# Attention over edges: the product of keys and queries stays in PSUM, and the values' product stands between the two score products

## The chip, the cores and the metric

The kernel runs on one core of one Trainium2 chip (trn2). The metric is the device time of one execution in microseconds, as the median of several runs. Engines are named as in the profile: PE is TensorE, DVE is VectorE, ACT is ScalarE, POOL is GpSimd, SP is SyncE; "q" behind a name means its sequencer, which issues DMAs.

## The reference

A network of four graph blocks over 6,250 nodes and 106,250 edges, 128 features wide, each block followed by a residual and a layer norm. The change is in the last one, attention over edges with 8 heads of 16:

```python
Q = (x @ WQ).reshape(N, H, dh)
K = (x @ WK).reshape(N, H, dh)
V = (x @ WV).reshape(N, H, dh)
Eh = (edge_attr @ WE).reshape(-1, H, dh)
score = K[src] * Q[dst] / jnp.sqrt(jnp.float32(dh)) * Eh
score = jnp.exp(jnp.clip(score.sum(-1, keepdims=True), -5.0, 5.0))
msg = V[src] * score
wV = jax.ops.segment_sum(msg, dst, num_segments=N)
Z = jax.ops.segment_sum(score, dst, num_segments=N)
h_attn = (wV / (Z + ATTN_EPS)).reshape(N, D)
```

## The kernel before

The edges are sorted by the tile (125 nodes) of their target node and laid out in 272 groups of 512 slots, four to each of 128 partitions. Groups beyond the edges that there are hold blanks. `attn` runs once, late in the program, as one loop over the groups on all engines at once: 34 trips of `Q` = 8 groups on DVE, PE and SP; on POOL it is written out. Most buffers form rings of `RING` = 4 groups.

For group g, in the order in which its data move:

- POOL (L748) issues four indirect DMAs; each gathers 128 rows of keys and values (1 KB each) from `kv_table` into `kv_r`. Before a group's first gather it waits for `attn_ready` of group g - 4.
- SP (L663) loads the group's 256 KB of edge terms into `eh_r`, also once `attn_ready` tells that group g - 4 is done, and (L650) the row of target nodes of group g + 4 into `row_b`.
- DVE makes the one-hots `oht_r` of group g + 2 from `row_b` (`q_one_hots`, L1564), and counts `q_hot`.
- PE (`q_of`, L868) waits for `q_hot`, multiplies these with the tile of queries into PSUM bank 6 + g % 2, and counts `q_rows`. So a group's queries stand in PSUM two laps before they are used.
- DVE: `times_q` (L1581) waits for the four gathers (`kv_in`) and for `q_rows`, and multiplies the keys with the queries. Before the change the product goes to `gath[:, 6 + q % 2]` in SBUF. `times_eh` (L1587) multiplies it with the edge terms in place, `head_sums` (L1591) sums the 16 features of each head, `clamp` (L1597) limits the sums and counts `score_ready`.
- ACT takes the exponent (L1135, `exp_done`). Ahead of it in its queue stand the one-hots of the target nodes for group g + 2 (L1119, L1123), which wait for `attn_sums` of group g - 2.
- DVE: `times_scores` (L1602), one lap later, multiplies the values with the exponent into `vs_r` and counts `attn_ready`.
- PE (`sums`, L876) waits for `attn_ready` and the one-hots and adds up the group per node in PSUM; in PE's order `sums` of group g - 1 stands behind `q_of` of group g + 2. DVE adds the result to the node sums three laps later (`add`, L1576).

Each engine works strictly in the order in which its part is written. DVE's order within a lap is `lap` (the lines from 1609 on). Instructions of DVE that depend on one another wait through `sch` (semaphore `score_chain`).

Of the kernel before, what the change touches and what calls it, by code (L numbers as in the profile page):

```python
# [19 lines left out]
ALU, ACT = mybir.AluOpType, mybir.ActivationFunctionType  # L20
# [3 lines left out]
N, E, D = 6250, 106250, 128  # L24
# [12 lines left out]
RING = 4  # L37
# [179 lines left out]
def program(nc, A):  # L217
    ctx = ExitStack()
    with ctx:
# [55 lines left out]
        ps = ctx.enter_context(nc.psum_tensor("ps", [P, 8, 512], F32))  # L275
# [123 lines left out]
        kv_r = part_of_big([P, RING, PER, 2 * D], NA * NODES_PAD)  # L399
        eh_r = part_of_big([P, RING, PER, D])  # L400
# [883 lines left out]
        def _(dve):  # L1284
            ch, sch = Chain(dve, dve_chain), Chain(dve, score_chain)
# [272 lines left out]
            def attn(n):  # L1558
# [3 lines left out]
                def q_one_hots(i, q):  # L1562
# [3 lines left out]
                                      .rearrange("p (u j) -> p j u", j=UNIT), part[0:NT, 0:1], None,  # L1566
                                      ALU.is_equal).then_inc(q_hot, 1)

                def quads(q):
                    return gath[:, 6 + q % 2, :].rearrange("p (k f) -> p k f", f=D)  # L1570

# [6 lines left out]
                def times_q(g, trip, q):  # L1578
                    dve.wait_ge(kv_in[q], 16 * PER * trip)
                    dve.wait_ge(q_rows, g + 1)  # L1580
                    sch.mark(dve.tensor_tensor(quads(q), kv_r[:, q, :, 0:D],  # L1581
                                               ps[:, 6 + q % 2, :].rearrange("p (k f) -> p k f", f=D), ALU.mult))

                def times_eh(trip, q):
                    dve.wait_ge(eh_in[q], 16 * trip)
                    sch.wait()
                    sch.mark(dve.tensor_tensor(quads(q), quads(q), eh_r[:, q, :, :], ALU.mult))  # L1587

                def head_sums(q):
                    sch.wait()  # L1590
# [9 lines left out]
                def times_scores(g, q):  # L1600
                    dve.wait_ge(exp_done, g + 1)
                    dve.tensor_tensor(vs_r[:, q, :, 0:D].rearrange("p k (h d) -> p k h d", d=DH),  # L1602
                                      kv_r[:, q, :, D:2 * D].rearrange("p k (h d) -> p k h d", d=DH),
                                      vs_r[:, q, :, D:SUMS_W].unsqueeze(3).to_broadcast([P, PER, HEADS, DH]),
                                      ALU.mult).then_inc(attn_ready, 1)

                def lap(i, first, last):
                    ch.trip(i, Q)
                    sch.trip(i, 3 * Q)
                    if not first:  # L1610
                        ch.k -= lag
                        at_ = tiles_of(DVE_E, ATT_D, i * Q - lag, Q)
                    else:
                        at_ = (0,) * lag + tuple(tiles_of(DVE_E, ATT_D, 0, Q - lag))
                    for q in range(Q):
                        g, r, trip = i * Q + q, q % RING, i * (Q // RING) + q // RING + 1
                        times_q(g, trip, r)
                        if not (last and q >= Q - 2):
                            q_one_hots(i + (q + 2) // Q, (q + 2) % Q)
                        times_eh(trip, r)  # L1620
                        head_sums(r)
                        clamp(r)
                        if not (first and q == 0):
                            times_scores(g - 1, (q - 1) % RING)
                        if not (first and q < lag):
                            add(g - lag, (q - lag) % RING, at_[q])
                q_one_hots(0, 0)
                q_one_hots(0, 1)
                laps(dve, TRIPS, lap)
                ch.k += lag  # L1630
                ch.leave(TRIPS, Q)
# [244 lines left out]
```

## Time and profile before

| | us |
|---|---|
| median of 3 runs | 11,246.82 |
| lowest and highest | 11,230.78, 11,254.05 |
| span of the profiled execution, first to last instruction | 10,395.6 |
| the attention loop in it | 8,817 to 10,301 |

The profiled execution is told by its span alone; the difference to the median, some 851 us, lies outside the first and the last instruction. A span is read against a span, and a run's time against a run's time. The page lists the instruction groups by busy time, with the idle time of the engine before them and what ended it. The stretches of the trace give each engine's busy time from one time to another, the time line every instruction with its start and duration. Gathers by POOL are rows of L748: the row is the time in which POOL makes the transfer's descriptors, not the transfer itself.

### The profile page before, as it was taken

Reading aid. Unit: us, or ns where it says so; the run is one execution under the profiler, and the core shown is the slowest. Engines: PE = TensorE matmul, PEld = TensorE weight load, DVE = VectorE, ACT = ScalarE, POOL = GpSimd, SP = SyncE. Lnnn points to the kernel's source line nnn. Section 1 sums busy time; section 2 is a strip of 40 time slices with the busy share of each in tenths; the row PEclk is TensorE's granted clock in tenths of the full one; section 3 lists DMA queues with packets and bytes.
Section 4 is the critical chain, followed back from the end, with each engine's and each line's share of the span. In section 5 each row is a group of like instructions: output and inputs, shape, how many; then the busy total and the mean of one; then the engine's idle time right before and its main releaser. Section 6 shows DMA issues by size and latency. Waiting matters only on the chain.

```text
span 10395.6 us, 235883 instructions
## 1 busy us (share of the span) xinstructions
PE 7622.6 (73%) x62128; PEld 6495.8 (62%) x62129; DVE 7083.8 (68%) x16991; ACT 3619.7 (35%) x7576; POOL 4980.3 (48%) x4705
## 2 busy tenths in 40 slices
PE   4799990388787887884689777777877875666664
PEld 3567660277675776763578676766766765556553
DVE  5577770266766667666666579789798797666664
ACT  0122220230612604404520454644645544444443
POOL 0677776337054072270036037056074173777772
PEclk7555555699899998996899899999999998666665
DMA  8767664997584884960599489598796894666666
GB/s 338 198 211 213 214 208 33 101 280 244 197 293 130 296 258 156 329 190 21 159 326 421 188 323 364 214 337 303 263 352 248 307 364 157 165 162 164 161 162 78
DMA packets 1747195, 2371.76 MB, mean 228 GB/s; under 512 B 516388, under 2 KB 1046151, under 8 KB 1746651
## 3 DMA queue, kind: packets, MB, share of 16 engines
q1 hardware_dynamic: 1292446, 1275.33, 39.4%
q0 software_dynamic: 318912, 1049.17, 31.1%
q10 hardware_dynamic: 135677, 45.42, 1.9%
q8 instruction: 64, 1.05, 0.0%
q14 instruction: 96, 0.79, 0.0%
HBM read 1485.10 MB, written 955.49 MB: 235 GB/s over the span
## 4 chain that ended last, share of the span: by engine, by line
PE 19%; DVE 8%; POOL 7%; issue 6%; ACT 4%; DMA 4%; SPq 2%; DVEq 2%; ACTq 0%; POOLq 0%
PE ps L836 8%; POOL big L748 6%; PE ps L858 5%; PE ps L855 4%; DVE gath L1516 3%; ACT gath L1109 3%; DMA big<-kv_table,src_at 2%; SPq L622 2%; ACT gath L1088 1%; DVE gath L1587 1%; DVE heads L1591 1%; ACT big L1241 0%; DMA big<-rec 0%; DVE gath L1602 0%; DVEq L509 0%
## 5 line engine op out<-in xcount | busy, mean ns | idle before, releaser
L738 POOL DMA_INDIRECT gath<-msg_units,unit_at_d x2176 | 2341.0, 1076 | 3287.8 <-DMA msg_units<-gath 2605.4
L858 PE MATMUL ps<-onehot,gath 128*128 128x125 f32 x17408 | 2476.3, 287 | 636.9 <-ACT gath L1109 356.1
L858 PEld LDWEIGHTS ps<-onehot,gath 128*128 128x128 f32 x17408 | 2118.7, 193 | 994.4 <-issue 536.9
L836 PE MATMUL ps<-big,onehot 125*128 x29376 | 1921.2, 223 | 713.1 <-DVE onehot L1477 466.9
L836 PEld LDWEIGHTS ps<-big,onehot 125*128 125x128 bf16 x29376 | 1806.3, 97 | 830.8 <-issue 788.0
L1088 ACT ACTIVATE gath<-ps 128x512 f32<-128x512 f32 x2448 | 1425.3, 597 | 1212.3 <-PE ps L836 1013.0
L1477 DVE TENSOR_SCALAR onehot<-row_b,part 125x512 bf16<-125x512 uint8 x2448 | 1136.4, 482 | 690.7 <-PE ps L836 686.4
L1509 DVE TENSOR_TENSOR onehot<-iota,node_d 128x500 f32<-128x500 f32 x2176 | 1464.7, 674 | 173.4 <-PE ps L858 109.7
L748 POOL DMA_INDIRECT big<-kv_table,src_at x1088 | 1085.5, 998 | 537.2 <-issue 291.8
L710 POOL DMA_INDIRECT rec<-big,idx_ring x832 | 973.6, 1170 | 282.8 <-issue 239.9
L1109 ACT ACTIVATE gath<-gath 128x512 f32<-128x512 f32 x1088 | 685.6, 630 | 941.6 <-DVE gath L1516 941.6
L1528 DVE TENSOR_TENSOR big<-big,ps 128x125 f32 x2176 | 608.9, 280 | 391.9 <-PE ps L858 383.0
L868 PE MATMUL ps<-big,weights 125*128 x2176 | 467.0, 382 | 397.5 <-DVE weights L1564 397.5
L1516 DVE TENSOR_TENSOR gath<-gath,big 128x512 f32<-128x512 f32 x1088 | 742.9, 683 | 21.4 <-DMA gath<-msg_units,unit_at_d 21.1
L868 PEld LDWEIGHTS ps<-big,weights 125*128 125x128 f32 x2176 | 404.7, 278 | 460.4 <-issue 460.3
L876 PE MATMUL ps<-gath,onehot 128*125 128x136 f32 x2176 | 515.7, 409 | 121.6 <-DVE gath L1602 110.3
L1160 ACT ACTIVATE big<-ps,feats 128x250 f32 x125 | 53.9, 470 | 1502.7 <-PE ps L923 1502.4
L1119 ACT ACTIVATE onehot<-iota,weights 128x125 f32<-128x125 f32 x1088 | 344.7, 388 | 659.5 <-PE ps L876 612.3
L876 PEld LDWEIGHTS ps<-gath,onehot 128*125 128x125 f32 x2176 | 451.6, 296 | 180.8 <-issue 137.5
L1581 DVE TENSOR_TENSOR gath<-big,ps 128x512 f32<-128x512 f32 x272 | 186.8, 687 | 527.3 <-DMA big<-kv_table,src_at 518.3
L816 PE MATMUL ps<-weights,big 128*128 128x128 f32 x1664 | 419.7, 432 | 94.6 <-DMA gath<-in_attr_t 55.1
L738 POOL DMA_INDIRECT big<-rec,unit_at_s x136 | 138.8, 1021 | 713.9 <-DMA rec<-gath 636.4
(218 smaller groups left out, 9000.0 us busy)
## 6 DMA issues: line engine op xcount, KB each, us to landing
msg_units<-gath SPq DMA_DIRECT2D x2176, 256.0 KB, 2.2
big<-ea_units SPq DMA_DIRECT2D x1088, 256.0 KB
ea_units<-rec SPq DMA_DIRECT2D x16, 4352.0 KB, 54.4
rec<-gath SPq DMA_DIRECT2D x272, 256.0 KB, 6.2
big<-rec SPq DMA_DIRECT2D x272, 256.0 KB, 3.8
big<-in_attr_t SPq DMA_DIRECT2D x208, 256.0 KB
rec<-big SPq DMA_DIRECT2D x1, 43296.0 KB, 152.1
gath<-msg_units,unit_at_d POOLq DMA_INDIRECT x2176, 5.3
```

Source lines behind the costliest of these rows:

```text
L710: pool.indirect_dma_start(rec, bass.IndirectOffsetOnAxis(ap=idx_ring[:, q, k:k + 1], axis=0), rec_r[:, q, k, :], None).then_inc(rec_out[q] ...
L738: pool.indirect_dma_start(att_slot(q) if way == "attr" else gath[:, q, :], None, units, bass.IndirectOffsetOnAxis(ap=unit_at[w][:, g:g + 1 ...
L748: pool.indirect_dma_start(kv_r[:, q, k, :], None, table["kv"], bass.IndirectOffsetOnAxis(ap=src_at[:, g * PER + k:g * PER + k + 1], axis=0))\
L836: ins = pe.matmul(ps[:, r, c], hots_t[0:NT, r, c], upper[0:NT, ds(at_[q] + b, D)], start=b == NA * NODES_PAD, stop=b == LOW)
L858: ins = pe.matmul(ps[:, RING + r, 0:NT], unit_ring[:, q, j, :], hots[:, r, j, :], start=j == 0, stop=j == UNIT - 1)
L868: last = pe.matmul(ps[:, 6 + q % 2, k * P:(k + 1) * P], oht_r[0:NT, q % 2, k, :], big[0:NT, ds(at_ + RE * NODES_PAD, P)], start=True, stop ...
L876: last = pe.matmul(ps[0:NT, q, 0:SUMS_W], hots[:, q, k, :], vs_r[:, q, k, :], start=k == 0, stop=k == PER - 1)
L1088: act.activation(unit_ring[:, q, :, :], ps[:, q % RING, :].rearrange("p (k f) -> p k f", f=D), ACT.Copy).then_inc(evicted, 1)
L1109: act.activation(gath[:, q, :], gath[:, q, :], ACT.Relu).then_inc(msg_ready, 1)
L1477: dve.tensor_scalar(hots_t[0:NT, r, :].rearrange("p (j u) -> p j u", u=P), row_b[0:NT, k, q % RING * GSLOTS:(q % RING + 1) * GSLOTS] .rear ...
L1509: dve.tensor_tensor(hots[:, r, :, :], iota[:, 0:NT].unsqueeze(1).to_broadcast([P, UNIT, NT]), node[w][:, ds(g * UNIT, UNIT)].unsqueeze(2). ...
L1516: dve.tensor_tensor(gath[:, q, :], gath[:, q, :], ea_r[:, q, :], ALU.add).then_inc(msg_sum, 1)
```

## The change

Three things change, all in DVE's part of `attn`; no other engine's instructions change. `times_q` writes its product back into the PSUM bank that it read the queries from. `times_eh` reads it there and writes `gath` in SBUF, from where the head sums go on as before. And in a lap `times_scores` of the group before moves up to stand between these two products, while the one-hots of group g + 2 move down behind `times_eh`: these release PE to overwrite the same bank.

```diff
+                def q_ps(q):
+                    return ps[:, 6 + q % 2, :].rearrange("p (k f) -> p k f", f=D)
...
-                    sch.mark(dve.tensor_tensor(quads(q), kv_r[:, q, :, 0:D],
-                                               ps[:, 6 + q % 2, :].rearrange("p (k f) -> p k f", f=D), ALU.mult))
+                    sch.mark(dve.tensor_tensor(q_ps(q), kv_r[:, q, :, 0:D], q_ps(q), ALU.mult))
...
-                    sch.mark(dve.tensor_tensor(quads(q), quads(q), eh_r[:, q, :, :], ALU.mult))
+                    sch.mark(dve.tensor_tensor(quads(q), q_ps(q), eh_r[:, q, :, :], ALU.mult))
...
                         times_q(g, trip, r)
+                        if not (first and q == 0):
+                            times_scores(g - 1, (q - 1) % RING)
+                        times_eh(trip, r)
                         if not (last and q >= Q - 2):
                             q_one_hots(i + (q + 2) // Q, (q + 2) % Q)
-                        times_eh(trip, r)
                         head_sums(r)
                         clamp(r)
-                        if not (first and q == 0):
-                            times_scores(g - 1, (q - 1) % RING)
```

DVE in a lap in the middle of the loop, before. The rows are, in order, the product with the queries, the one-hots (written to a part of `weights`), the product with the edge terms, head sums, clamp, the values' product (written to a part of `gath`), and the addition to the node sums (two rows).

```order
L1581 TENSOR_TENSOR gath<-big,ps 128x512 [waits q_rows,kv_in0]
L1564 TENSOR_SCALAR weights<-row_b,part 125x512 [waits q_row_in6]
L1587 TENSOR_TENSOR gath<-gath,big 128x512 [waits score_chain,eh_in0]
L1591 TENSOR_REDUCE heads<-gath 128x32 [waits score_chain]
L1597 TENSOR_SCALAR heads<-heads 128x32 [waits score_chain]
L1602 TENSOR_TENSOR gath<-big,gath 128x4x128 [waits exp_done]
L1576 ISA [waits dve_chain,attn_sums]
L1576 TENSOR_TENSOR big<-big,ps 125x136
```

The same lap after, three lines further down in the file:

```order
L1584 TENSOR_TENSOR ps<-big,ps 128x512 [waits q_rows,kv_in0]
L1604 TENSOR_TENSOR gath<-big,gath 128x4x128 [waits exp_done]
L1589 TENSOR_TENSOR gath<-ps,big 128x512 [waits score_chain,eh_in0]
L1564 TENSOR_SCALAR weights<-row_b,part 125x512 [waits q_row_in6]
L1593 TENSOR_REDUCE heads<-gath 128x32 [waits score_chain]
L1599 TENSOR_SCALAR heads<-heads 128x32 [waits score_chain]
L1579 ISA [waits dve_chain,attn_sums]
L1579 TENSOR_TENSOR big<-big,ps 125x136
```

The values' product, with its wait for the exponent of the group before, has moved from the sixth place to the second, and the one-hots from the second to the fourth; the first product now writes `ps`, and the product with the edge terms reads it.

DVE in the last lap and behind it, where there are no one-hots left to make, before:

```order
L1581 TENSOR_TENSOR gath<-big,ps 128x512 [waits q_rows,kv_in3]
L1587 TENSOR_TENSOR gath<-gath,big 128x512 [waits score_chain,eh_in3]
L1591 TENSOR_REDUCE heads<-gath 128x32 [waits score_chain]
L1597 TENSOR_SCALAR heads<-heads 128x32 [waits score_chain]
L1602 TENSOR_TENSOR gath<-big,gath 128x4x128 [waits exp_done]
L1576 ISA [waits dve_chain,attn_sums]
L1576 TENSOR_TENSOR big<-big,ps 125x136
L1602 TENSOR_TENSOR gath<-big,gath 128x4x128 [waits exp_done]
```

And after:

```order
L1584 TENSOR_TENSOR ps<-big,ps 128x512 [waits q_rows,kv_in3]
L1604 TENSOR_TENSOR gath<-big,gath 128x4x128 [waits exp_done]
L1589 TENSOR_TENSOR gath<-ps,big 128x512 [waits score_chain,eh_in3]
L1593 TENSOR_REDUCE heads<-gath 128x32 [waits score_chain]
L1599 TENSOR_SCALAR heads<-heads 128x32 [waits score_chain]
L1579 ISA [waits dve_chain,attn_sums]
L1579 TENSOR_TENSOR big<-big,ps 125x136
L1604 TENSOR_TENSOR gath<-big,gath 128x4x128 [waits exp_done]
```

Here too the values' product of the group before moves up; that of the last group stands alone behind the loop in both.

## Rows read from the trace of the kernel before

**Rows 1.** The page: its first line, and L1581 among the costliest groups.

```profile
span 10395.6 us, 235883 instructions
...
L1581 DVE TENSOR_TENSOR gath<-big,ps 128x512 f32<-128x512 f32 x272 | 186.8, 687 | 527.3 <-DMA big<-kv_table,src_at 518.3
```

**Rows 2.** Stretches: from:to, length, busy us (count) by engine, clock, DMA, GB/s.

```profile
8830.00:10130.00 1300.00, 876.87 (x3973) 767.18 (x3973) 835.72 (x1739) 541.71 (x1494) 996.56 (x996) 0.68 0.63 163
10130.00:10300.00 170.00, 90.04 (x350) 78.35 (x350) 75.85 (x158) 44.73 (x123) 79.06 (x83) 0.57 0.94 103
```

**Rows 3.** Waits, 8830 to 10130 us: waiter <- releaser: us, times, longest.

```profile
DVE gath L1581 <- DMA big<-kv_table,src_at: 441.3, 220, 6.2
...
POOL big L748 <- issue: 269.3, 884, 0.3
...
POOL big L748 <- DVE gath L1602: 34.1, 112, 0.3
```

**Rows 4.** Groups by line, 8830 to 10130 us: busy us, mean ns | idle before.

```profile
L748 POOL DMA_INDIRECT big<-kv_table,src_at x996 | 997.0, 1001 | 303.5 <-issue 269.3 <-DVE gath L1602 34.1
...
L1581 DVE TENSOR_TENSOR gath<-big,ps 128x512 f32<-128x512 f32 x249 | 171.0, 687 | 447.0 <-DMA big<-kv_table,src_at 441.3 <-issue 5.5
L1587 DVE TENSOR_TENSOR gath<-gath,big 128x512 f32<-128x512 f32 x249 | 170.8, 686 | 0.0
L1591 DVE TENSOR_REDUCE heads<-gath 128x32 f32<-128x512 f32 x249 | 170.8, 686 | 8.6
L1602 DVE TENSOR_TENSOR gath<-big,gath 128x512 f32<-128x512 f32 x248 | 169.6, 684 | 0.0
L1564 DVE TENSOR_SCALAR weights<-row_b,part 125x512 f32<-125x512 uint8 x249 | 122.7, 493 | 0.0
...
L1597 DVE TENSOR_SCALAR heads<-heads 128x32 f32<-128x32 f32 x249 | 50.5, 203 | 8.7
```

**Rows 5.** Time line at 9083 us: start us, us, engine, line, operation.

```profile
9082.77 0.69 DVE L1581 TENSOR_TENSOR gath<-big,ps 128x512 f32<-128x512 f32 x1 [1.03 <-DMA big<-kv_table,src_at]
9083.37 0.48 DVE L1564 TENSOR_SCALAR weights<-row_b,part 125x512 f32<-125x512 uint8 x1
9083.77 0.68 DVE L1587 TENSOR_TENSOR gath<-gath,big 128x512 f32<-128x512 f32 x1
9083.90 1.37 POOL L748 DMA_INDIRECT big<-kv_table,src_at  x1 [0.30 <-issue]
...
9085.30 0.68 DVE L1602 TENSOR_TENSOR gath<-big,gath 128x512 f32<-128x512 f32 x1
9085.57 1.23 POOL L748 DMA_INDIRECT big<-kv_table,src_at  x1 [0.30 <-issue]
```

**Rows 6.** Time line at 9432 us, a lap with a quick landing.

```profile
9431.69 0.69 DVE L1591 TENSOR_REDUCE heads<-gath 128x32 f32<-128x512 f32 x1
9432.18 0.95 POOL L748 DMA_INDIRECT big<-kv_table,src_at  x1 [0.30 <-issue]
...
9433.38 0.58 SPq L663 DMA_DIRECT2D big<-rec  x1
...
9435.03 0.69 DVE L1581 TENSOR_TENSOR gath<-big,ps 128x512 f32<-128x512 f32 x1 [1.64 <-DMA big<-kv_table,src_at]
...
9435.93 1.00 POOL L748 DMA_INDIRECT big<-kv_table,src_at  x1 [0.30 <-issue]
9436.03 0.68 DVE L1587 TENSOR_TENSOR gath<-gath,big 128x512 f32<-128x512 f32 x1
```

**Rows 7.** Time line at 9086 us, an earlier load of edge terms.

```profile
9086.14 0.58 SPq L663 DMA_DIRECT2D big<-rec  x1
...
9089.19 0.69 DVE L1581 TENSOR_TENSOR gath<-big,ps 128x512 f32<-128x512 f32 x1 [3.00 <-DMA big<-kv_table,src_at]
```

**Rows 8.** Waits, 10130 to 10300 us.

```profile
POOL big L748 <- DVE gath L1602: 54.5, 18, 7.4
```

**Rows 9.** DMA queues, 10140 to 10280 us: packets, MB, share of 16 engines.

```profile
q0 software_dynamic: 3515, 9.61, 81.3%
```

## The prediction, made before the changed kernel ran

> **What bounds the kernel now.** I read the page first, then the attention loop by stretches, by waits, by line and in order of time. The page says that L1581, DVE's first product of the attention loop, is preceded by 527.3 us of idle time, ended by the gather of keys and values [rows 1]. The stretches place all that the diff touches: the loop lies between 8817 and 10301 us, some 1,484 of the 10,395.6 us, and it has two parts [rows 2]. Up to 10130 us POOL issues 996 gathers, four to a group, so 249 groups in 1,300 us or 5.22 us each. In the last 170 us it issues 83, some 21 groups at 8 us, and the DMA engines are 94% busy against 63% before.
>
> In the first part DVE waits 441.3 us for gathers, 220 times; POOL waits for nobody more than 0.3 us at a time, and all its idle time comes to 303.5 us over 996 gathers, 0.30 each [rows 3, 4]. Where the view of waits names "DVE gath L1602" as POOL's releaser there, the wait is no longer than the 0.30 us that stand before every other gather, so it is no wait. POOL's own rate bounds this part: 1.001 us of gather and 0.305 us before it, four times, is 5.22 us. DVE needs 0.687 + 0.493 + 0.686 + 0.686 + 0.203 + 0.684 = 3.44 us for a group, without one small addition [rows 4], PE 877/249 = 3.5 us [rows 2]. Whatever DVE saves or loses for itself within that margin changes nothing.
>
> What can be changed is the 1.001. Of the 996 gathers 734 take 0.94 to 0.96 us, 108 take up to 1.10 and 154 take more, 1.26 on average (counted over the POOL rows of the time line between 8830 and 10130 us). The long ones have company. A gather that starts 0.13 us into L1587 takes 1.37 us, one that starts 0.27 us into L1602 takes 1.23 [rows 5]; one that starts 0.49 us into the reduction L1591 takes 0.95 [rows 6]. In both long cases the gather ends 0.83 to 0.85 us behind the DVE instruction's end, as though it had been held until then. A second kind starts up to 0.3 us ahead of such an instruction and ends 0.90 us after that one's start: 1.00 us for the one that leads L1587 by 0.10 [rows 6]. Counted in the same way: 100 gathers start within L1587, mean 1.163; 123 within L1602, mean 1.140; 124 within the one-hots L1564, mean 1.018, most of them followed by L1587; 231 within L1581 or L1591, mean 0.948; 418 with DVE idle, 0.946. L1587 and L1602 read both inputs from SBUF. L1581 has one input in PSUM and L1591 has one input, and they hold nothing. The excess over 0.946 comes to 996 x 0.055 = 55 us: some 22 from L1587, 9 around L1564, 24 from L1602. This is all that the first part can give.
>
> The Trainium skill ("SBUF — State Buffer", Who interferes with whom) states that a VectorE instruction with two SBUF inputs contends with a GpSimd instruction that reads SBUF, and one with at most one SBUF input does not. By that rule, the trace agrees: 1.37 and 1.23 against 0.95.
>
> **The change part by part.** (1) The product of keys and queries writes PSUM instead of SBUF. No row has a DVE write to PSUM. Its nearest rows are 687 ns with a PSUM input and 684 ns without PSUM; I take 687, with ends at 0.49 (the one-hots' row) and twice the row, 1.37. Even then it costs nothing: 447.0/249 = 1.8 us a group lie idle ahead of L1581 [rows 4]. (2) The product with the edge terms reads PSUM and one SBUF operand, the form of L1581: 687 for 686 ns, nothing in DVE time, but it stops holding gathers: between -22 and -31 us (whether the one-hots' 9 belong to L1587 or to L1564 itself can't be told, since L1587 follows 0.40 us behind).
>
> The Trainium skill ("VectorE: DVE Perf Modes", The TRN2 errata) gives a VectorE instruction a fixed 120 cycles from PSUM and 58 from SBUF, which speaks against this edit. By it 272 x 65 ns would be an estimated 18 us of DVE time; 687 against 684 ns show none of it, and either lies in idle time.
>
> (3) The values' product moves from 2.53 us to 0.60 us behind the start of L1581 (9085.30 and 9083.37 against 9082.77 [rows 5]: it takes the one-hots' place). It still has two SBUF inputs, so its 24 us don't vanish but are dealt anew, and this decides the result. Let 0 be the end of a group's fourth gather. Undisturbed, the next ones start at 0.30, 1.55, 2.79, 4.04. L1581 starts when the fourth has landed. In 112 of the 249 laps that is before 2.0, as in [rows 6] at 1.91 (9435.03 - 9433.12): the product would run from 2.51 to 3.19 and the third gather, starting 0.28 into it, would be held to 1.23 as in [rows 5]: +0.28 us. Landings from 2.5 to 2.75 put it between two gathers: nothing. Dealt evenly over the 1.25 us between two gathers, a product of this length costs 0.17 us a lap (the two holds summed over all offsets: 0.59 squared / 2 and 0.27 squared / 2, over 1.25); before, it cost 24/249 = 0.10.
>
> (4) With the product, its signal to SyncE and POOL comes 1.93 us earlier, and so does the next load of edge terms. Now it is issued some 0.2 us behind the end of the fourth gather and the gather lands quickly [rows 6]. Where it was issued 0.66 us ahead of that end, the landing took 2.39 us [rows 7]; 29 such laps mean 2.59, and five with 1.1 to 2.4 us ahead lie between 2.53 and 3.11. With the change it comes ahead by 0.9 to 1.9 us (landing + 0.60 + 0.68 + 0.19 against the next fourth end 4.98 to 5.26 later). So landings should move to about 2.6, into the gap of (3). I put the product at 0.05 to 0.17 us a lap, and take 0.10, 25 us.
>
> (5) The one-hots move from 0.60 to 1.81 behind L1581's start, with PE's q_of behind them by as much; q_rows is wanted two laps later, and in the first part L1581's waits are the gathers' [rows 3]. PE then reaches the sums some 0.85 us later, the ACT one-hots too; the exponent, behind them in ACT's queue, ends near 3.4 of the lap and is wanted at 0.60 of the next, 2.4 us to spare. If that cover went, every lap would lengthen. Standing alone, the one-hots may hold gathers themselves: 0 to 0.06 us a lap, I take 0.02, 5 us.
>
> (6) L1591 waits for L1587's end with the one-hots between: a gap of 0.03 us less, in idle time. At the end of the stage the same instructions stand in another order: nothing. In the second part POOL waits 54.5 us for L1602, longest 7.4 [rows 8]. An earlier signal would serve it, but the DMA engines are full, the gathers' queue alone 81% [rows 9]; I give it 0 to -4 us, take -1.
>
> Sum: 55 us of holds become 25 + 5, so -25, and -1: -26 us. The profiled execution's own time is its span, 10,395.6 us, and about 851 us outside it up to the median of 11,246.8, which the change doesn't touch; its runs spread by 23 us. 11,246.8 - 26 = 11,221 us.
>
> **The rivals.** *The product falls clear of the gathers nearly always* (for: landings near 2.6 hold themselves there; against: their spread, 1.8 to over 5): -45 to -57, 11,190 to 11,202 us.
> *One hold for another*: landings stay as now, the product takes 0.2 us in nearly half of the laps and what L1587 gave is spent: -10 to +8, 11,237 to 11,255.
> *The ring wait*, which 34.1 + 54.5 us of POOL waiting for L1602 suggest [rows 3, 8]: it would give up to 50 us if the second part were bound by the signal. The full DMA engines speak against it.
> *Slower*: landings settle below 2.2, the product holds a gather in every lap (0.28) and the one-hots, alone now, another for 0.10: (0.38 - 0.22) x 249 = +40, 11,287 us. It decides when over three laps in four are held by both. For: 112 laps land so now. Against: (4).
> *That only a two-port write matters.* The Trainium skill ("SBUF — State Buffer", same section) also says that `tensor_tensor` was not seen to stall DMA, inferring that descriptor generation needs the write interface. As a mechanism here: the gathers' length then follows something else and nothing changes, 11,247 us. The 1.37 and 1.23 us speak against that.
>
> **How the numbers follow.** Forecast (-10 to -44) 45%, clear 17%, one hold for another 20%, no effect 4%, ring wait 3%, slower 10%, something unseen 1%. The measurement can tell about 0.2%, 22 us. Faster by more than that: clear, ring and two thirds of the forecast, 0.50. Slower: 0.10. Same: 0.40. The range leaves out the slower case and the last of the clear one: 11,191 to 11,257 us.
>
> **What would show it.** In the profile after: L748's mean in the steady part near 0.975 us instead of 1.001, no gather over 1.1 us that starts within the product with the edge terms, long ones only at the values' product and perhaps the one-hots; L1581's counterpart near 0.69 us; groups at 5.12 us. It is wrong if the edge product still holds gathers, if the write to PSUM takes over 2 us, if DVE begins to wait for PE, or if the gathers' landing doesn't move.

## The result: slower where it was timed, quicker elsewhere

| | before | changed |
|---|---|---|
| median of the runs | 11,238.8 us (4 runs, 11,230.8 to 11,254.1) | 11,283.0 us (4 runs, 11,272.9 to 11,288.9) |
| ratio | | 1.0041 [1.0029, 1.0053] |
| profiled execution | span 10,395.6 us | 11,272.9 us, span 11,271.2 us |

The change costs 0.41%, some 45 us, where 26 us less were forecast; the time lies above the range. The profile of the changed kernel contradicts the prediction before any instruction is looked at. Its page begins:

```profile
span 11271.2 us, 235883 instructions
...
L858 PE MATMUL ps<-onehot,gath 128*128 128x125 f32 x17408 | 2516.3, 299 | 965.3 <-issue 403.4
...
L748 POOL DMA_INDIRECT big<-kv_table,src_at x1088 | 1057.4, 972 | 958.5 <-DVE gath L1604 484.1
L868 PE MATMUL ps<-big,weights 125*128 x2176 | 435.9, 364 | 1102.6 <-DVE weights L1564 938.3
...
L1604 DVE TENSOR_TENSOR gath<-big,gath 128x512 f32<-128x512 f32 x272 | 189.0, 695 | 569.4 <-ACT gath L1135 498.1
```

The span is 1.7 us shorter than the time of its execution. The span of before [rows 1] was 851 us shorter than the timed runs beside it. The spans of the 18 further profiles below all lie within 3 us of the time of their own execution. So the profile of before shows an execution of some 10,397 us, unlike the ones that were timed, and the 851 us do not lie outside its first and last instruction. The kernel has **two conditions**: in each batch of runs below, which shared one chip, the median of the kernel before was either 10,384 to 10,412 us (here "the 10.4 ms condition") or 11,100 to 11,239 us ("the 11.2 ms condition"), and stayed there. The first timing, of both kernels, was of the second kind and the profile of before of the first. No profile of before in the 11.2 ms condition exists, so the profile after can't be set against [rows 1 to 9] to learn what the change did; most of the difference between them is the condition.

What the attention loop looks like there is seen in two-microsecond stretches of the changed kernel, inside the loop (it runs from 9300 to 11,161 us there). The columns are those of [rows 2]: from:to, length, busy us (count) of PE, PEld, DVE, ACT and POOL, granted clock, DMA share, GB/s.

```profile
9694.00:9696.00 2.00, 0.51 (x5) 0.30 (x3) 0.12 (x1) 0.00 (x0) 1.57 (x2) 1.00 0.74 195
9696.00:9698.00 2.00, 0.00 (x0) 0.00 (x0) 0.00 (x0) 0.00 (x0) 1.27 (x2) 0.92 0.44 107
9698.00:9700.00 2.00, 0.00 (x0) 0.00 (x0) 0.00 (x0) 0.03 (x1) 0.00 (x0) 0.50 0.31 76
9700.00:9702.00 2.00, 0.00 (x0) 0.00 (x0) 0.00 (x0) 1.97 (x6) 0.00 (x0) 0.50 0.00 0
9702.00:9704.00 2.00, 0.04 (x1) 0.04 (x1) 1.87 (x4) 1.97 (x6) 0.91 (x1) 0.50 0.00 0
```

DVE and PE are at rest first, POOL goes on for a while, then no engine is busy until ACT starts again. The granted clock falls from 1.00 only after PE has come to rest, so it does not start the stall. The time line of the same place (start us, us, engine, line, operation, idle time before and what ended it):

```profile
9688.10 1.09 PE L876 MATMUL ps<-gath,onehot 128*125 128x136 f32 x8
...
9696.63 0.94 POOL L748 DMA_INDIRECT big<-kv_table,src_at  x1 [0.30 <-issue]
...
9699.97 1.27 ACT L1119 ACTIVATE onehot<-iota,weights 128x125 f32<-128x125 f32 x4 [10.51 <-remote]
...
9702.13 0.69 DVE L1604 TENSOR_TENSOR gath<-big,gath 128x512 f32<-128x512 f32 x1 [8.02 <-ACT gath L1135]
...
9703.09 0.94 POOL L748 DMA_INDIRECT big<-kv_table,src_at  x1 [5.52 <-DVE gath L1604]
```

PE issued the sums that free ACT's one-hots at 9688.1 us. ACT goes on at 9699.97, after 10.51 us of rest; behind it come the exponent, DVE's product with it (8.02 us of rest) and, behind that product's signal, POOL (5.52 us). In the waits of the loop, 9330 to 11,150 us (waiter <- releaser: us, times, longest), this is a chain of three with nearly the same count:

```profile
ACT onehot L1119 <- remote: 861.7, 88, 10.9
...
DVE gath L1604 <- ACT gath L1135: 495.0, 89, 9.3
POOL big L748 <- DVE gath L1604: 474.7, 89, 8.8
...
POOL big L748 <- issue: 312.4, 974, 2.0
```

"Remote" means that the trace has no record of the releaser. POOL waited for nobody in the first part of the loop of before [rows 3]; here it waits 474.7 us, about once in every third group.

### The profile page after: what moved, and what is told of

It reads as the page before. It is cut to its first block, busy times and chain, and to the rows that moved or that the text cites. A ratio compares the mean times of both kernels' runs of the same rounds, so it can differ in the third digit from the quotient of the medians.

```text
span 11271.2 us, 235883 instructions
## 1 busy us (share of the span) xinstructions
PE 7467.7 (66%) x62128; PEld 6516.2 (58%) x62129; DVE 7088.4 (63%) x16991; ACT 3595.9 (32%) x7576; POOL 4910.4 (44%) x4705
## 4 chain that ended last, share of the span: by engine, by line
PE 22%; issue 9%; another core or an unknown queue 8%; DVE 5%; ACT 4%; SPq 2%; DMA 1%; DVEq 1%; ACTq 1%; POOL 0%; POOLq 0%
PE ps L836 8%; PE ps L858 7%; PE ps L855 4%; SPq L622 2%; ACT onehot L1119 1%; DVE gath L1516 1%; PE ps L868 1%; PE ps L876 1%; ACT gath L1109 1%; ACT gath L1088 1%; DVE gath L1589 1%; ACT big L1241 0%; ACT onehot L1123 0%; ACT gath L1135 0%
## 5 line engine op out<-in xcount | busy, mean ns | idle before, releaser
L738 POOL DMA_INDIRECT gath<-msg_units,unit_at_d x2176 | 2304.0, 1059 | 3690.6 <-DMA msg_units<-gath 2611.6
L858 PE MATMUL ps<-onehot,gath 128*128 128x125 f32 x17408 | 2516.3, 299 | 965.3 <-issue 403.4
L858 PEld LDWEIGHTS ps<-onehot,gath 128*128 128x128 f32 x17408 | 2258.6, 208 | 1222.9 <-issue 954.9
L748 POOL DMA_INDIRECT big<-kv_table,src_at x1088 | 1057.4, 972 | 958.5 <-DVE gath L1604 484.1
L868 PE MATMUL ps<-big,weights 125*128 x2176 | 435.9, 364 | 1102.6 <-DVE weights L1564 938.3
L1119 ACT ACTIVATE onehot<-iota,weights 128x125 f32<-128x125 f32 x1088 | 343.2, 386 | 1232.2 <-remote 875.0
L1604 DVE TENSOR_TENSOR gath<-big,gath 128x512 f32<-128x512 f32 x272 | 189.0, 695 | 569.4 <-ACT gath L1135 498.1
L1463 DVE STREAM_SHUFFLE row_b<-row_b 128x512 int32<-128x512 int32 x612 | 447.4, 731 | 0.0
L816 PEld LDWEIGHTS ps<-weights,big 128*128 128x128 f32 x1664 | 360.1, 319 | 120.8 <-issue 119.6
```

Source lines behind the costliest of these rows:

```text
L738: pool.indirect_dma_start(att_slot(q) if way == "attr" else gath[:, q, :], None, units, bass.IndirectOffsetOnAxis(ap=unit_at[w][:, g:g + 1 ...
L748: pool.indirect_dma_start(kv_r[:, q, k, :], None, table["kv"], bass.IndirectOffsetOnAxis(ap=src_at[:, g * PER + k:g * PER + k + 1], axis=0))\
L816: pe.matmul(ps[:, 4 + r, c], attr_t[:, q, c], weight("we"), start=True, stop=True)
L858: ins = pe.matmul(ps[:, RING + r, 0:NT], unit_ring[:, q, j, :], hots[:, r, j, :], start=j == 0, stop=j == UNIT - 1)
L868: last = pe.matmul(ps[:, 6 + q % 2, k * P:(k + 1) * P], oht_r[0:NT, q % 2, k, :], big[0:NT, ds(at_ + RE * NODES_PAD, P)], start=True, stop ...
```

## The experiments

All kernels of a batch ran on one chip with the kernel before; the condition is read from before's own time there. Confidence intervals of ratios are 95%.

### In the 10.4 ms condition: which part acts

**The kernel before, again.** 

> The kernel before, unchanged, to get a profile that can be laid beside that of the changed kernel: the first profile spans 10,395.6 us while its timed runs take 11,239, and the changed kernel's profile spans 11,271 with a time of 11,273, and was 483 us later already at the start of the attention loop, where nothing is changed. Theory A (two conditions of the device, the first profile was taken in the faster one): this profile spans about 11,237 us, the attention loop is near 1,816 us (1,860 of the changed kernel less 44) and not 1,484, and PE's completions arrive late in bursts as they do in the changed kernel. Theory B (profiling changes it): it spans 10,396 again. Time ratio 1.000.

Measured: 10,382.6 us, ratio 1.0000 [0.9991, 1.0009], span 10,379.5 of an execution of 10,381.2 us. Nothing of 851 us lies outside the span.

**The order alone**: the product stays in SBUF.

```diff
                         times_q(g, trip, r)
+                        if not (first and q == 0):
+                            times_scores(g - 1, (q - 1) % RING)
+                        times_eh(trip, r)
                         if not (last and q >= Q - 2):
                             q_one_hots(i + (q + 2) // Q, (q + 2) % Q)
-                        times_eh(trip, r)
                         head_sums(r)
                         clamp(r)
-                        if not (first and q == 0):
-                            times_scores(g - 1, (q - 1) % RING)
```

> The changed order alone, with the product of keys and queries in SBUF as before. Theory A (the order costs: the values' product in second place makes DVE wait for the exponent of the group before, or the later one-hots delay PE's sums): 40 to 50 us slower than before, like the changed kernel. Rival (the write to PSUM, or PE and DVE on one bank, costs): within 10 us of before.

Measured: 10,382.0 us, 1.0004 [0.9995, 1.0013].

**The product in PSUM, the values' product in its old place** (the one-hots stay behind the edge product):

```diff
                         times_q(g, trip, r)
-                        if not (first and q == 0):
-                            times_scores(g - 1, (q - 1) % RING)
                         times_eh(trip, r)
...
                         clamp(r)
+                        if not (first and q == 0):
+                            times_scores(g - 1, (q - 1) % RING)
```

> The product stays in PSUM and the one-hots stand behind the product with the edge terms, but the values' product keeps its old place behind the clamp. Theory A1 (the early values' product costs by waiting for the exponent): within 10 us of before. Theory A2 (the later one-hots, and with them PE's q_of and sums, cost): 40 us slower as the changed kernel. Rival (PSUM): 40 us slower too, then told apart by the order alone.

Measured: 10,344.4 us, 0.9966 [0.9954, 0.9978].

**The values' product ahead of the edge product, in SBUF, with the one-hots left second:**

```diff
                             q_one_hots(i + (q + 2) // Q, (q + 2) % Q)
+                        if not (first and q == 0):
+                            times_scores(g - 1, (q - 1) % RING)
                         times_eh(trip, r)
...
                         clamp(r)
-                        if not (first and q == 0):
-                            times_scores(g - 1, (q - 1) % RING)
```

> The values' product moves ahead of the product with the edge terms, the one-hots stay in second place, the product of keys and queries stays in SBUF. Theory A1 (waiting for the exponent costs): 30 to 50 us slower. Theory A2 (the later one-hots cost): within 10 us of before, or some us faster, since PE gets its one-hots as early as before and the sums earlier.

Measured: 10,383.2 us, 1.0000 [0.9991, 1.0009].

**The changed kernel, and before once more**, in a batch of their own:

> The changed kernel, unchanged, beside runs of before on one device. The device of the last four kernels ran before in 10,384 us, that of the first timing in 11,239. Theory A (the change's effect depends on the device: where POOL's gathers bound the loop, it gains what the product with the edge terms no longer holds, less what the values' product in its new place holds; on the slower device something else bounds it and the change costs): if before takes about 10,384 us here, the changed kernel takes 10,340 to 10,375, the loop's gathers have a mean of 0.96 to 0.99 us; if before takes about 11,240, it is again 40 us slower. Theory B (the change costs 40 us wherever it runs): 10,424 us.

> The kernel before on the same device as the run beside it, for its profile. If this is the slower device, theory A expects an attention loop of some 1,816 us in it, with DVE, ACT and POOL waiting several us at a time as in the changed kernel's first profile; if the faster one, a loop of 1,465 to 1,470 us.

Measured: 10,348.9 us against 10,391.6, 0.9964 [0.9950, 0.9977]. The same kernel that lost 0.41% gains 0.36%. Two orders with the product in SBUF change nothing, and with the product in PSUM it makes no difference where the values' product stands: in this condition the PSUM bank is the whole effect that the times can tell.

**Four kernels sent to meet the other condition; it did not come:**

> The kernel before, for a profile on whatever device this is. On a slower device (before in 11,100 to 11,240 us): the attention loop takes 1,780 to 1,820 us, and it has the pattern of the changed kernel's first profile there, that is engines at rest for 8 to 10 us every third lap or so, their restart together with the end of the gather queue's packets. Theory S1 (on such devices the signals of PE, ACT and DVE are late while POOL issues gathers without a pause, so whatever lets POOL issue faster makes the stalls no shorter): its gathers have a mean of about 1.00 us and the stalls are fewer or shorter than in the changed kernel's. On the faster device: a loop of 1,470 us.

> The changed kernel beside before on this device. Slower device: 1.003 to 1.005 of before, as in the first timing. Faster device: 0.9964.

> The changed order alone, product in SBUF. On the slower device theory S1 (what costs there is that gathers are no longer held): within 0.1% of before. Rival S2 (the earlier signal to POOL, or the wait for the exponent in second place, lengthens the stalls): 1.003 to 1.005 of before. On the faster device 1.000.

> The product in PSUM with the values' product in its old place. On the slower device theory S1: 1.002 to 1.005 of before, since its gathers are held as little as in the kernel whose two products both read PSUM, which took 1.0030 there. Rival S2: within 0.1% of before. On the faster device 0.9966.

Measured: before 10,388.5 (10,384.5 in the runs beside it), changed 10,347.3 (0.9967 [0.9956, 0.9979]), order alone 10,379.5 (0.9995 [0.9985, 1.0004]), product in PSUM with the old place 10,344.4 us (0.9968 [0.9956, 0.9981]). They repeat the above on another chip and say nothing on the slower case. Their traces are the ones that show why. The gathers of the steady part, 8840 to 10080 us (busy us, mean ns | idle before), in before, the order alone and the product in PSUM of the first batch:

```profile
L748 POOL DMA_INDIRECT big<-kv_table,src_at x946 | 952.4, 1007 | 288.2 <-issue 261.7 <-DVE gath L1602 26.5
```
```profile
L748 POOL DMA_INDIRECT big<-kv_table,src_at x949 | 952.3, 1003 | 289.2 <-issue 284.9 <-DVE gath L1602 4.3
```
```profile
L748 POOL DMA_INDIRECT big<-kv_table,src_at x979 | 943.4, 964 | 298.2 <-issue 265.3 <-DVE gath L1604 32.9
```

and, with the DVE groups that the change touches, in the changed kernel of this batch:

```profile
L748 POOL DMA_INDIRECT big<-kv_table,src_at x972 | 944.0, 971 | 296.1 <-issue 289.1 <-DVE gath L1604 7.0
...
L1584 DVE TENSOR_TENSOR ps<-big,ps 128x512 f32<-128x512 f32 x243 | 169.0, 695 | 394.7 <-DMA big<-kv_table,src_at 347.3 <-issue 39.1 <-PE ps L868 8.3
...
L1604 DVE TENSOR_TENSOR gath<-big,gath 128x512 f32<-128x512 f32 x243 | 166.3, 684 | 1.0 <-ACT gath L1135 0.9
L1589 DVE TENSOR_TENSOR gath<-ps,big 128x512 f32<-128x512 f32 x243 | 165.8, 682 | 0.0
```

The idle time per gather is 0.30 us in all four; the mean gather is 1.007, 1.003, 0.964 and 0.971 us. A gather 0.12 us into the edge product is not held any more, one 0.15 us into the values' product is (time line of the changed kernel):

```profile
8948.55 0.68 DVE L1589 TENSOR_TENSOR gath<-ps,big 128x512 f32<-128x512 f32 x1
8948.67 0.95 POOL L748 DMA_INDIRECT big<-kv_table,src_at  x1 [0.30 <-issue]
...
9019.61 0.69 DVE L1604 TENSOR_TENSOR gath<-big,gath 128x512 f32<-128x512 f32 x1 [0.94 <-ACT gath L1135]
9019.76 1.36 POOL L748 DMA_INDIRECT big<-kv_table,src_at  x1 [0.30 <-issue]
```

### The holds taken away, and put back

**No product with two SBUF inputs left**: on the kernel with the product in PSUM and the old place, ACT writes the exponent a second time, into a PSUM bank, and the values' product reads it there.

```diff
+                        act.activation(ps[:, 4 + q % 2, 0:PER * HEADS], heads[:, q, :],
+                                       ACT.Exp, scale=1.0 / DH ** 0.5).then_inc(exp_done, 1)
...
-                                      vs_r[:, q, :, D:SUMS_W].unsqueeze(3).to_broadcast([P, PER, HEADS, DH]),
+                                      ps[:, 4 + q % 2, 0:PER * HEADS].rearrange("p (k h) -> p k h", k=PER)
+                                      .unsqueeze(3).to_broadcast([P, PER, HEADS, DH]),
```

> On top of the kernel with the product in PSUM and the values' product in its old place (9966 ten-thousandths of before on the faster device): ACT writes the exponent a second time, into PSUM banks 4 and 5, and the values' product reads it there, so that it too has only one SBUF input. Theory (only DVE instructions with two SBUF inputs, and perhaps the one-hots, hold POOL's gathers): the holds at the values' product vanish, what is left sits at the one-hots; the mean of a gather in the steady part is under 0.955 us, the time on the faster device 10,318 to 10,340 us, that is 45 to 65 us under before. ACT has 0.25 us more a lap, hidden. Rival (what was gained came from the order of instructions or from the landing times, not from operands): 10,344 us as without this edit.

**More holds**: the kernel before with one more product a group at the end of the lap, whose result nobody reads; and the same with its second input in PSUM, which adds the DVE time but no holds.

```diff
+                        dve.tensor_tensor(spare, kv_r[:, r, :, 0:D], eh_r[:, r, :, :], ALU.mult)
```
```diff
+                        dve.tensor_tensor(spare, kv_r[:, r, :, 0:D], ps[:, 4, :].rearrange("p (k f) -> p k f", f=D), ALU.mult)
```

> The kernel before with one more product per group on DVE, at the lap's end, whose result nobody reads: keys times edge terms, both in SBUF. Theory: DVE has 1.8 us a lap to spare, so its own 0.6 us costs nothing, but it holds gathers that start within it: +15 to +45 us over before. Rival (a gather's length has nothing to do with DVE's operands): within 5 us of before, as the next one.

> The same additional product, at the same place, but its second input is PSUM bank 4 instead of the edge terms in SBUF. Theory: within 8 us of before, the gathers that start within it take 0.945 us. Rival (DVE time itself counts): slower by as much as the one with two SBUF inputs.

This batch met the 11.2 ms condition: before 11,100.1 us. Measured: no holds 11,127.9 us (1.0030 [1.0017, 1.0042]); more holds 11,066.0 (0.9972 [0.9963, 0.9981]); more DVE time without holds 11,114.9 (1.0018 [1.0009, 1.0027]). The kernel with the additional held gathers is the quickest of the four. The two unread products are also the cleanest pair on what holds: they stand at the same place and last as long, and only the second input differs. With it in SBUF the 77 gathers that start within the product take 1.36 us on average, with it in PSUM 172 take 0.948, none over 0.95 (of the same 1000 gathers as in the table below). In the time line, SBUF first (from the kernel's trace in the other condition), then PSUM:

```profile
9022.68 0.69 DVE L1629 TENSOR_TENSOR gath<-big 128x512 f32<-128x512 f32 x1
9022.79 1.39 POOL L748 DMA_INDIRECT big<-kv_table,src_at  x1 [0.30 <-issue]
...
9604.69 0.68 DVE L1629 TENSOR_TENSOR gath<-big,ps 128x512 f32<-128x512 f32 x1
9604.81 0.95 POOL L748 DMA_INDIRECT big<-kv_table,src_at  x1 [0.30 <-issue]
```

**The same in the other condition:**

> The kernel before, for a profile on whatever device this is. On a slower device (11,100 to 11,240 us): an attention loop of 1,780 to 1,820 us with engines at rest for 8 to 10 us every third lap, ended together with the end of the gather queue's packets. On the faster device: a loop of 1,470 us, as twice before.

> Both products read one input in PSUM: the edge terms' from the bank, the values' from a second copy of the exponent in banks 4 and 5. On the faster device, where this was not yet run: the gathers' mean falls under 0.955 us and the time is 10,318 to 10,340 us, 0.994 to 0.996 of before, against 0.9967 with the edge product alone. Rival (the gain is not that of the holds): 0.9967 as without this edit. On the slower device 1.003 again.

> The kernel before with one product more per group, both inputs in SBUF, result unread. On the faster device, where this was not yet run: 15 to 45 us slower than before, 1.0015 to 1.004, since it holds more gathers. Rival (holds don't set the loop's rate there either): 1.000. On the slower device 0.997 again.

This batch met the 10.4 ms condition: before 10,411.7 us (10,405.0 as a run of its own). No holds: 10,362.1 us (0.9956 [0.9942, 0.9969]); more holds: 10,460.4 (1.0049 [1.0034, 1.0064]). Both signs are turned. The gathers of the steady part, no holds first, then more holds:

```profile
L748 POOL DMA_INDIRECT big<-kv_table,src_at x984 | 941.1, 956 | 299.8 <-issue 273.0 <-DVE gath L1606 26.8
```
```profile
L748 POOL DMA_INDIRECT big<-kv_table,src_at x910 | 963.3, 1059 | 277.3 <-issue 271.8 <-DVE gath L1602 5.5
```

984 gathers against 910 in the same 1,240 us.

**The two parts once more**, with the hope for the 11.2 ms condition:

> The changed order alone, product in SBUF, on whatever device this is. On a slower device (before in 11,100 to 11,240 us): within 0.1% of before if what costs there is that gathers are no longer held; 1.003 to 1.005 of before if the order costs there. On the faster device 1.000, as twice before.

> The product in PSUM with the values' product in its old place, on whatever device this is. The order alone took 0.9987 of before on a slower device (before 11,224 us), so what costs there should be the product in PSUM: 1.003 to 1.006 of before on a slower device. If it is within 0.1% there, neither part costs by itself and the cost is that of both together. On the faster device 0.9967, as twice before.

The order alone met it: 11,212.2 against 11,224.4 us, 0.9987 [0.9977, 0.9997]. The product in PSUM did not: 10,340.9 against 10,390.7 us, 0.9956 [0.9941, 0.9970]. Together with the first result, 1.0041 against 0.9987, this points to the product in PSUM as what costs in that condition. It is not shown: the two ratios come from two batches, and the product in PSUM alone was not run there.

### What the traces of the 11.2 ms condition show

The gathers between 9330 and 10900 us, of the changed kernel, the order alone, no holds, more holds, and more DVE time without holds:

```profile
L748 POOL DMA_INDIRECT big<-kv_table,src_at x923 | 898.3, 973 | 671.9 <-DVE gath L1604 401.4 <-issue 270.6
```
```profile
L748 POOL DMA_INDIRECT big<-kv_table,src_at x954 | 953.6, 1000 | 616.8 <-DVE gath L1602 337.7 <-issue 279.0
```
```profile
L748 POOL DMA_INDIRECT big<-kv_table,src_at x941 | 893.6, 950 | 677.6 <-DVE gath L1606 401.4 <-issue 276.2
```
```profile
L748 POOL DMA_INDIRECT big<-kv_table,src_at x979 | 1035.0, 1057 | 536.3 <-issue 287.2 <-DVE gath L1602 249.1
```
```profile
L748 POOL DMA_INDIRECT big<-kv_table,src_at x952 | 931.1, 978 | 640.2 <-DVE gath L1602 368.0 <-issue 272.3
```

The means of one gather are what they are in the other condition (0.973 and 0.971 for the changed kernel, 1.057 and 1.059 with more holds). What is different is the idle time. Taken over the same 1000 gathers of each trace, the 9th to the 1008th, counted over POOL's rows (a stall is a wait of over 0.7 us; in this stretch there is none in any trace of the 10.4 ms condition):

| condition, kernel | length, us | in gathers | between them | stalls |
|---|---|---|---|---|
| 10.4 ms, before | 1312 | 1008 | 304 | 0 |
| 10.4 ms, changed | 1275 | 971 | 304 | 0 |
| 10.4 ms, product in PSUM, old place | 1267 | 963 | 304 | 0 |
| 10.4 ms, no holds | 1261 | 956 | 304 | 0 |
| 10.4 ms, more holds | 1362 | 1058 | 304 | 0 |
| 11.2 ms, order alone | 1651 | 1000 | 651 | 97, 376 us |
| 11.2 ms, changed | 1699 | 973 | 726 | 94, 449 us |
| 11.2 ms, no holds | 1668 | 950 | 718 | 91, 438 us |
| 11.2 ms, more holds | 1594 | 1057 | 537 | 56, 249 us |
| 11.2 ms, more DVE time | 1646 | 980 | 666 | 61, 380 us |

In the upper half the time between gathers is a constant, and each microsecond of holds is a microsecond of the loop. In the lower half less time in the gathers goes, by and large, with more in stalls (950 and 973 us with 438 and 449, 980 and 1000 with 380 and 376, 1057 with 249): from the order alone to the changed kernel 27 us come off the gathers and 75 us go on between them. That is where the loss stands. From the first gather to the last the loop takes 1803 and 1861 us, 58 longer, where the ratios differ by 0.54% or 61 us. Within one batch, from more holds to no holds: 1752 to 1823, 71 us, where the times differ by 62; from more holds to more DVE time: 49 us, and 49.

**What a stall waits for.** The traces also record when each engine's signals were given. In the changed kernel's trace of the 10.4 ms condition, over the stretch of the table, all 248 recorded signals of PE's sums stand 0.01 us behind the end of the matmul that gives them, and so do all 251 of `q_of`. In the 11.2 ms condition 217 signals of the sums have a record; measured from the last such matmul that had ended, their median is 5.5 us and 151 come over 3 us late. The 639 recorded signals of ACT and DVE in the changed kernel's stretch all stand 0.01 us behind their instruction. So among the signals that have a record it is PE's alone that come late, and the rest of the chain waits for them. In the case shown, the sums end at 9689.19; PE's next signals are recorded at 9699.83, 9699.92 and 9700.01, for sums, `q_of` and sums, 0.09 us apart, and ACT starts at 9699.97. Ahead of the loop, where the slower condition has already cost 483 us, 679 of PE's 6,058 recorded signals are over 1 us late, and none of 6,540 in the quick one.

| 11.2 ms, kernel | signals of the sums recorded | over 3 us late | rests of ACT ahead of L1119 over 6 us | ended near a packet's end | near one with a pause behind it |
|---|---|---|---|---|---|
| order alone | 214 | 125 | 91 | 70 | 41 |
| changed | 217 | 151 | 84 | 65 | 56 |
| no holds | 238 | 157 | 90 | 55 | 40 |
| more holds | 215 | 101 | 53 | 29 | 14 |
| more DVE time | 234 | 148 | 74 | 27 | 19 |

Why PE's signals come late is not shown. One candidate is the gathers' traffic. "Near" in the table means that ACT starts between 0.3 us before and 1.0 us after the end of the last packet of the gathers' queue. But of all instants of these stretches 0.50 to 0.54 lie as close, so in the last three rows the count is about what chance gives, or less. Near a packet behind which the queue pauses for over 1 us lie 0.05 to 0.11 of the instants, and more of the rests than that. So there is a link, but it doesn't account for most of the stalls outside the changed kernel; a kernel that fills the loop with other DMA traffic and no gathers would test it.

Another candidate is the recording of the trace: the changed kernel's trace of the 11.2 ms condition holds 101,877 records of semaphore signals, that of the 10.4 ms condition 185,991. Whether recording takes part in the delay, and whether late signals of ACT or DVE are among the records that are missing, no run here tells.

Why one condition has this and the other not is **open**, and so is why more holds mean fewer stalls (56 against 94). That a held POOL gives the queue time to run empty by itself would fit; nothing here separates it from others. Chip numbers don't settle it either: the first two batches, quick, and the order alone at the end, slow, carry the same one. The slower condition is also not the attention's alone: the loop begins at 9300 us of the span and not at 8817, before any line of the change has run.

## Why the prediction was wrong, point by point

- **The step that failed** is the last of the sum: "The profiled execution's own time is its span, 10,395.6 us, and about 851 us outside it". No profile here has more than some 3 us outside its span. The 851 us were the mark of another condition, and they took with them the statement that everything rested on, "POOL's own rate bounds this part". It bounds the loop of the profile; in the timed runs of the first result POOL stalls for 449 us over 1000 gathers, behind signals of PE that come late. That the sign turned in that condition could not be read from the profile of before.
- **The sum itself held where it was made.** In the 10.4 ms condition: forecast -26 us, measured -37 and -43 (10,384.5 to 10,347.3, 10,391.6 to 10,348.9). L748's mean: forecast near 0.975, measured 0.971 and 0.972. A group of four gathers: forecast 5.12 us, measured 5.10 and 5.11. The landing, from the end of a group's fourth gather to the start of the product that waits for it: forecast about 2.6 us, measured 2.76 (median), from 2.10 before; the order alone moves it as far.
- **What was undersized** is a term that the sum kept: it let the values' product hold 25 us instead of 24. Over 1000 gathers, before (taken again) has 62 us of holds: 24 within the edge product, 7 within the one-hots, 30 within the values' product. The changed kernel has 25: 22 within the values' product (88 gathers, mean 1.20) and 3 for gathers that start within the edge product shortly ahead of the one-hots. So 28 us came from the edge product and the one-hots, where the sum had 26, and some 7 from the values' product, where it had none; the five traces of before in this condition spread from 55 to 65 us, so the second figure is not firm. Against the order alone (57 us, of them 32 within the edge product and 25 within the values' product) the PSUM bank takes 29 off the first and 3 off the second.
- **The write to PSUM** takes 695 ns, the reading product 682. In the 10.4 ms condition neither matters: the margin is L1584's 394.7 us of idle time over 243 groups. The Trainium skill ("VectorE: DVE Perf Modes", The TRN2 errata) has 120 fixed cycles for reading PSUM and 58 for SBUF. The trace doesn't bear it out here: the edge product takes 682 ns with an input in PSUM and took 686 with both in SBUF.
- **The cover held in this condition**: DVE waits 8.3 us for PE and 1.0 us for the exponent in the steady part. In the other it is gone: the exponent that had "2.4 us to spare" is waited for 495 us.
- **That two SBUF inputs are what holds** is shown by taking them away one after the other: 1.007 us with both products, 0.964 and 0.971 with one, 0.956 with none, and 1.059 with a third added; and by the two unread products above, 1.36 against 0.948 us. The holds of one product are not independent of the other: with the edge product's input in PSUM and the old place, the values' product itself holds only 7 to 11 us (three traces) instead of 24 to 30 (five). In the kernel without either, 10 us of excess are left, at the one-hots: 43 gathers that start in them have a mean of 1.028 (3.5 us), and the rest is at gathers that start 0.3 to 0.5 us ahead of them. The Trainium skill ("SBUF — State Buffer", Who interferes with whom) says that two SBUF inputs contend, that one does only in the modes that take both ports, and that `tensor_tensor` was not seen to stall DMA; these runs agree with the first and not with the last, for indirect DMAs that POOL issues. Whether the one-hots run in such a mode no run here shows.
- **The second part of the loop** did not change: the last 80 gathers take 145 and 147 us in the changed kernel and 147 to 157 in the five traces of before in the 10.4 ms condition. The ring wait as a gain of up to 50 us is refuted.
- **The slower rival** had nearly the right number, 11,287 us, by luck: its mechanism needed landings under 2.2 us. They are 2.76 us where the profile's reasoning holds, and 10.9 (median) in the condition that was timed.

## The version to keep

In the 10.4 ms condition the kernel without two-input products in SBUF (the exponent in PSUM as well) and the one with the product in PSUM and the old place are the best, at 0.9956 [0.9942, 0.9969] and 0.9968 to 0.9956; the intervals don't tell them apart, nor from the changed kernel at 0.9964 and 0.9967. In the 11.2 ms condition the kernel without such products costs 0.30%. There the additional unread product gained 0.28% and the order alone 0.13%, but that additional product costs 0.49% in the other condition. No version that was timed in both gains in both; of these the order alone is the only one that costs in neither.

## What to carry to other kernels

Set the profile's span against the timed runs before reading anything in it: here they differed by 8%, the profile was of another condition, and its bound was not the bound of what was timed. Where POOL's issue of indirect DMAs is the bound, DVE products with both inputs in SBUF lengthen it, and one input in PSUM removes that for the product concerned (682 for 686 ns; writing it there cost 695 for 687). An edit that speeds up issuing can lose where something else stops the queue, so time it on several chips before believing either sign.

## What the hardware showed unexpectedly

- One and the same kernel takes 10,384 to 10,412 or 11,100 to 11,239 us (medians), in each batch only one of them. In the longer one the engines of the attention loop rest together, some 89 times between 9330 and 11,150 us, with ACT waiting 9.8 us on average (861.7/88).
- In that condition the recorded signals of PE come late, with a median of 5.5 us behind the sums and several at once, while those of ACT and DVE stand 0.01 us behind their instructions as in the other.
- The one-hots, with one SBUF input of bytes and 0.48 to 0.49 us long, hold gathers too: mean 1.028 us for those that start in them, up to 1.20, against 0.946.
- 272 additional DVE products of about 0.7 us made the whole kernel 34 us quicker in one condition (11,066.0 against 11,100.1 us) and 49 us slower in the other (10,460.4 against 10,411.7).
